# Four-stage block on one core: row scalings of the first stage on ScalarE, and new order tables for the state loops

## The reference

```python
x = x + layernorm(L0_attn(layernorm(x)))     # state-space layer
x = x + layernorm(L0_ffn(layernorm(x)))      # 8 experts, top 2, and a shared one
x = x + layernorm(L1_attn(layernorm(x)))     # differential attention
x = x + layernorm(L1_ffn(layernorm(x)))      # attention and experts with mixed weights

def layernorm(x): return (x - mean(x)) / sqrt(var(x) + 1e-5)   # over the 128 values of a row

# L0_attn, 256 channels d, 16 states n
u, z = split(x @ W_in.T)
uc = silu(conv1d(u, 3 taps) + conv_b)
B, C, dt = split(uc @ W_xproj.T);  delta = softplus(dt @ W_dt.T + b_dt)
h[n, t] = exp(delta * A[n]) * h[n, t-1] + delta * uc * B[n];  y = sum_n h[n] * C[n] + uc * D
out = (y * silu(z)) @ W_out.T

# L0_ffn, hidden size 512
combine = top-2 of softmax(x @ gate_w.T), normalized
out = sum_e combine[e] * (gelu(x @ W1[e] + b1[e]) @ W2[e] + b2[e]) + shared expert
```

## Time and profile before

| what | value |
|---|---|
| median of three runs | 2823.01 us |
| the profiled execution | 2826.37 us, of which the span is 2824.6 |
| mean granted TensorE clock | 0.876 of full speed |
| PE busy | 2196.3 us (78%), 15570 instructions |
| PEld busy | 1492.3 us (53%) |
| DVE busy | 2127.1 us (75%), 3677 instructions |
| ACT busy | 1699.0 us (60%), 2627 instructions |
| POOL busy | 1528.9 us (54%), 1343 instructions |
| L1300, VectorE's reduction of 128x1024 in the attention, x512 | mean 1215 ns |
| L791, TensorE's first up product of 128x512, x288 | mean 419 ns |
| ACT_TABLE_LOAD, x108 in the program | 1283 ns each |

### The profile page before, as it was taken

How to read it: one execution, slowest core, us unless ns; L and a number is a source line. 1 busy time by engine, 2 the same in 40 slices (tenths; PEclk the granted TensorE clock), 3 DMA queues, 4 the chain that set the end, 5 groups by cost and what they waited for, 6 DMA issues and landing times.

```text
span 2824.6 us, 42372 instructions
## 1 busy us (share of the span) xinstructions
PE 2196.3 (78%) x15570; PEld 1492.3 (53%) x15570; DVE 2127.1 (75%) x3677; ACT 1699.0 (60%) x2627; POOL 1528.9 (54%) x1343
## 2 busy tenths in 40 slices
PE   2433788588589697989889888989896799739877
PEld 1101456255356475656556566656664568536665
DVE  4999978978978514999999999999998431572344
ACT  5353666477457344989888888888894134212422
POOL 0435323523433202878987887788788524553146
PEclk7555889698689898999999999999997899869988
DMA  3000000000000000110000000011010000000000
GB/s 108 0 0 0 1 0 1 1 1 1 19 1 1 18 6 12 34 25 23 24 24 24 24 24 23 24 30 28 24 35 23 1 1 1 1 15 1 1 1 16
DMA packets 32032, 42.06 MB, mean 15 GB/s; under 512 B 8897, under 2 KB 18130, under 8 KB 31442
## 3 DMA queue, kind: packets, MB, share of 16 engines
q1 hardware_dynamic: 31826, 39.34, 5.2%
HBM read 12.05 MB, written 2.10 MB: 5 GB/s over the span
## 4 chain that ended last, share of the span: by engine, by line
PE 37%; DVE 35%; ACT 12%; issue 8%; POOL 7%; SPq 0%; DMA 0%; POOLq 0%; ACTq 0%; DVEq 0%
DVE MA L1300 11%; PE ps L862 7%; DVE WB L1309 5%; PE ps L791 3%; ACT HR L763 3%; PE ps L793 2%; PE ps L792 2%; PE ps L1161 2%; PE ps L1132 2%; PE ps L1985 2%; DVE lnb L317 2%; DVE BIG L336 2%; ACT BIG L448 2%; DVE BIG L342 2%; PE ps L1144 2%
## 5 line engine op out<-in xcount | busy, mean ns | idle before, releaser
L1300 DVE TENSOR_REDUCE MA<-ps 128x1 f32<-128x1024 f32 x512 | 606.3, 1215 | 42.6 <-PE ps L1132 38.5
L420 POOL TENSOR_TENSOR MA<-MA,BIG 128x1024 f32<-128x1024 f32 x128 | 299.0, 2357 | 544.1 <-DVE BIG L342 544.1
L1228 ACT ACTIVATE WB<-ps,MA 128x1024 f32<-128x1024 f32 x461 | 513.4, 1117 | 114.9 <-DVE MA L1300 102.6
L1132 PE MATMUL ps<-BIG 96*128 96x512 f16 x1024 | 316.1, 391 | 95.3 <-ACT WB L1228 84.3
L1380 POOL TENSOR_SCALAR WB<-WB,MA 128x384 f32<-128x384 f32 x256 | 371.1, 1450 | 8.5
L862 PEld LDWEIGHTS ps<-WB,HR 128*128 128x128 f32 x2304 | 291.6, 202 | 33.8 <-issue 16.7
L862 PE MATMUL ps<-WB,HR 128*128 128x128 f32 x2304 | 300.4, 288 | 8.7 <-DVE acc L707 8.5
L763 ACT ACTIVATE HR<-ps,b 128x512 f32<-128x512 f32 x288 | 190.2, 686 | 148.9 <-PE ps L793 148.0
L1732 POOL TENSOR_TENSOR BIG<-MA,BIG 128x512 f32<-128x512 f32 x128 | 132.9, 1048 | 229.6 <-PE ps L1971 76.1
L1144 PE MATMUL ps<-ident,WB 128*128 128x128 f32 x1640 | 226.2, 282 | 9.8 <-DVE WB L1309 5.7
L1383 POOL TENSOR_TENSOR WB<-WB 128x384 f32<-128x384 f32 x205 | 209.3, 1021 | 17.1
(11 more groups left out here) (294 smaller groups left out, 4962.3 us busy)
## 6 DMA issues: line engine op xcount, KB each, us to landing
BIG<-BIG SPq DMA_DIRECT2D x192, 64.0 KB, 2.0
BIG<-MA SPq DMA_DIRECT2D x192, 64.0 KB, 2.0
WB<-w_dram SPq DMA_DIRECT2D x1, 2304.0 KB, 14.9
X<-x_dram SPq DMA_DIRECT2D x4, 512.0 KB, 12.6
HR<-w_dram SPq DMA_DIRECT2D x1, 2048.0 KB, 9.5
out_dram<-X SPq DMA_DIRECT2D x4, 512.0 KB, 3.2
BIG<-wqkv_dram SPq DMA_DIRECT2D x1, 1536.0 KB, 6.2
WB<-w_dram SPq DMA_DIRECT2D x2, 512.0 KB, 5.1
```

What stands on the lines that cost most here:

```text
L420: e.tensor_tensor(yy[:, c, :], yy[:, c, :], db[n % 2][c], ALU.add).then_inc(*p_my.up(b, n, c))
L1132: x = e.matmul(ps[s][:, 512 * h:512 * h + 512], stack[q % 2][0:96, 0, 2 * pp + s, 128 * i:128 * i + 128], stack[q % 2][0:96, 1, 2 * pp + s ...
L1228: e.activation(P_of(n, s), ps[s][:, :], ACT.Exp, bias=L[:, 2 * s + pp:2 * s + pp + 1], scale=1.0, accum_out=L[:, 4 + 2 * s + pp:5 + 2 * s ...
L1300: e.tensor_reduce(L_of(n)[:, c:c + 1], ps[s][:, :], AX, ALU.max, negate=True).then_inc(*v_amx.up(n, s))
```

## The change

The sixteen groups of eight L317 in the first stage go from VectorE to ScalarE. ScalarE computes factor * x + shift in one activation (Identity with per-row scale and bias), for which GpSimd makes the shift, -mean * factor, with two more operations on 128x8 values after the 1/sqrt. The semaphores of the norms change their owner (`v_mln` becomes `a_mln`, `v_fln` becomes `a_fln`), and a few waits are added that guard the small tiles. All tables of planned times are new, so pieces move on every engine. The attention and the last block keep their L317 on VectorE; they gain only guards at their first use. A part of the diff (of the tables, two of thirteen):

```diff
-IN_AT = {"stats": 59.8, "norm": 72.1, "tr": 75.4, ..., "conv1": 98.3, "silu": 101.5, "wx": 104.5, ...}
+IN_AT = {"stats": 61.3, "norm": 68.5, "tr": 75.3, ..., "conv1": 91.5, "silu": 96.7, "wx": 101.6, ...}
-LOOP_AT = {"tb": -3.75, "scan1": 2.72, "scan0": 4.94, "th": 7.2, ..., "z": 20.8, "zK": 1.47, "za": -0.43}
+LOOP_AT = {"tb": -0.76, "scan1": 2.84, "scan0": 4.1, "th": 7.79, ..., "z": 18.68, "zK": -4.54, "za": 4.8}
...
+        def scale_shift(e, s):
+            rstd(e, s).then_inc(*pool_own.up())
+            e.tensor_scalar(s[:, :, 7:8], s[:, :, 6:7], -1.0, None, ALU.mult).then_inc(*pool_own.up())
+            e.wait_ge(*pool_own.now())
+            return e.tensor_tensor(s[:, :, 8:9], s[:, :, 7:8], s[:, :, 9:10], ALU.mult)
+
+        def normalized(e, s, src, dst):
+            for j in range(8):
+                i = e.activation(dst[:, j, :], src[j], ACT.Identity, bias=s[:, j, 8:9], scale=s[:, j, 9:10])
+            return i
...
         def front_dve(e, b):
             yield in_at(b, "stats")
+            last = m_order.index((b, "in")) - 1
+            if last >= 0:
+                e.wait_ge(*p_mrs.at(*m_order[last]))
             stats(e, st["m"], ...).then_inc(*v_mst.up(b, "in"))
-            yield in_at(b, "norm")
-            e.wait_ge(*p_mrs.at(b, "in"))
-            if b >= 2:
-                e.wait_ge(*p_mx.at(b - 2))
-            norms(e, st["m"], [tile_of(b, j) for j in range(8)], lnb[0]).then_inc(*v_mln.up(b, "in"))
...
         def front_pool(e, b):
             e.wait_ge(*v_mst.at(b, "in"))
-            rstd(e, st["m"]).then_inc(*p_mrs.up(b, "in"))
+            last = m_order.index((b, "in")) - 1
+            if last >= 0:
+                e.wait_ge(*a_mln.at(*m_order[last]))
+            scale_shift(e, st["m"]).then_inc(*p_mrs.up(b, "in"))
...
         def front_act(e, b):
+            yield in_at(b, "norm")
+            e.wait_ge(*p_mrs.at(b, "in"))
+            if b >= 2:
+                e.wait_ge(*p_mx.at(b - 2))
+            normalized(e, st["m"], [tile_of(b, j) for j in range(8)], lnb[0]).then_inc(*a_mln.up(b, "in"))
...
         def back_act(e, b):
+            yield out_at(b, "norm")
+            e.wait_ge(*p_mrs.at(b, "out"))
+            normalized(e, st["m"], [lnb[0][:, j, :] for j in range(8)], lnb[0]).then_inc(*a_mln.up(b, "out"))
...
         def moe_act(e, b):
+            yield f_at(b, "norm")
+            e.wait_ge(*p_frs.at(b, "in"))
+            if b:
+                e.wait_ge(*p_fx.at(b - 1))
+            normalized(e, st["f"], [tile_of(b, j) for j in range(8)], lnb[1]).then_inc(*a_fln.up(b, "in"))
             yield f_at(b, "tr", 1.2)
...
+            yield f_at(b, "rnorm")
+            e.wait_ge(*p_frs.at(b, "out"))
+            normalized(e, st["f"], [acc[:, j, :] for j in range(8)], lnb[1]).then_inc(*a_fln.up(b, "out"))
```

More of the change, by code:

```diff
@@ L96 @@
[L96 to L103, removed]
@@ L104 @@
-F_AT3 = {"stats": 0.08, "norm": 4.85, "tr": 8.6, "flo": 10.35, "gate": 11, "top": 12.79, "e": 15.58, "wts": 19.21,
-         "cT": 19.28, "k": 16.29, "K": 6.29, "up": 0.56, "dn": 6.03, "dnj": 0.78, "ge": 0.82, "done": 8.09,
-         "add": 1.73, "end": 132.4, "rnorm": 139, "x": 148.2}
+IN_AT0 = {"stats": -0.58, "norm": 1.89, "tr": 7.85, "u": 12.93, "tap0": 16.6, "tap1": 15.13, "conv0": 14.42,
+          "conv1": 22.1, "silu": 21.6, "wx": 23.8, "bc1": 26.4, "bc2": 27.8, "wdt0": 29.5, "wdt1": 35, "exp": 36.6,
+          "sp0": 40.2, "ln0": 39, "dl0": 42.9, "sp1": 40.1, "ln1": 49.1, "dl1": 51.2, "du": 52.2}
@@ new lines @@
+F_AT0 = {"stats": 2.45, "norm": 5.53, "tr": 7.35, "flo": 9.3, "gate": 8.76, "top": 17.44, "e": 20.7, "wts": 19.24,
+         "cT": 25.9, "k": 17.92, "K": 8.73, "up": 0.9, "dn": 3.84, "dnj": 1.42, "ge": 1.13, "done": 10.47,
+         "add": 11.98, "end": 186.4, "rnorm": 193.8, "x": 189.7}
+F_AT2 = {"stats": -1.4, "norm": 7.56, "tr": 12.5, "flo": 13.31, "gate": 17.42, "top": 22.6, "e": 24.1, "wts": 26.6,
+         "cT": 26.4, "k": 17.68, "K": 8.28, "up": 0.65, "dn": 6.1, "dnj": 0.26, "ge": 0.92, "done": 11.51,
+         "add": 7.2, "end": 172.8, "rnorm": 173.7, "x": 177.8}
@@ L107 @@
+F_AT3 = {"stats": -0.54, "norm": 3.84, "tr": 1.58, "flo": 14.87, "gate": 11.29, "top": 11.76, "e": 15.6, "wts": 9.85,
+         "cT": 19.46, "k": 13.36, "K": 6.65, "up": 1.05, "dn": 12.94, "dnj": 0.67, "ge": 0.43, "done": -0.33,
+         "add": 7.21, "end": 136.6, "rnorm": 137.1, "x": 135.5}
 F_AT = [F_AT0, F_AT0, F_AT2, F_AT3]
-LOOP_AT = {"tb": -3.75, "scan1": 2.72, "scan0": 4.94, "th": 7.2, "add": 9.43, "da": 0.34, "rows0": 4.86,
-           "rows1": 12.09, "z": 20.8, "zK": 1.47, "za": -0.43}
@@ L429, in back_pool @@
             e.wait_ge(*v_mst.at(b, "out"))
-            rstd(e, st["m"]).then_inc(*p_mrs.up(b, "out"))
+            last = m_order.index((b, "out")) - 1
+            if last >= 0:
+                e.wait_ge(*a_mln.at(*m_order[last]))
+            scale_shift(e, st["m"]).then_inc(*p_mrs.up(b, "out"))
             yield out_at(b, "x")
-            e.wait_ge(*v_mln.at(b, "out"))
+            e.wait_ge(*a_mln.at(b, "out"))
             xb = X[:, 8 * b:8 * b + 8, :]
@@ L657, in moe_dve @@
             yield f_at(b, "stats")
+            if b:
+                e.wait_ge(*p_frs.at(b - 1, "out"))
             stats(e, st["f"], [tile_of(b, j) for j in range(8)], {0: p_mx.at(b)}).then_inc(*v_fst.up(b, "in"))
-            yield f_at(b, "norm")
-            e.wait_ge(*p_frs.at(b, "in"))
-            if b:
-                e.wait_ge(*p_fx.at(b - 1))
-            norms(e, st["f"], [tile_of(b, j) for j in range(8)], lnb[1]).then_inc(*v_fln.up(b, "in"))
             yield f_at(b, "flo")
@@ L1272, in attend_dve @@
                     if b == 0:
[L1273 removed]
+                        e.wait_ge(*p_mrs.at(NB - 1, "out"))
                     for j in range(8):
@@ L1365, in attend_pool @@
                 e.wait_ge(*v_ast[0].at(b))
+                if b == 0:
+                    e.wait_ge(*a_mln.at(NB - 1, "out"))
                 rstd(e, st["m"]).then_inc(*p_ars[0].up(b))
```

53 lines of the change are left out of this document (29 added, 24 removed).

## The result

The changed kernel takes 2796.94 us (median of 9 runs, 2792.45 to 2802.04) against 2820.41 (median of 9, 2808.29 to 2827.39) for the kernel before. The ratio is 0.9922, with a 95% interval of 0.9905 to 0.9938: 22 us faster by the ratio, 23 by the medians. The prediction had 2826 as its likeliest time, a range of 2802 to 2845, and a chance of 0.51 for no difference.

A forecast was written before the change was run, and what follows sets the result against it. VectorE's freed time was held worthless in expert stretches; in handovers only the serial chain to L802 counts. Terms +1.7 - 1.3 - 0.8 + 7 - 10 + 0.5 + 4 + 1.8 = +2.9 on median 2823.0 gave 2826 us; range 2802 to 2845.

The forecast's parts named there:

- The group on ScalarE: Eight scalings on ScalarE, forecast at 3.2 us, bounds 2.2 and 3.8; 1.1 us longer than VectorE's group.
- The pair where GpSimd is free: GpSimd's added negation and product per group: 0.6 us where VectorE is idle, 1.0 where it is busy.
- The opening: First group, at 24.01 us, is on the chain: 0.6 + 1.1 = +1.7 us.
- The input group beside the second expert: Next batch's input group between third and fourth Gelu of the second expert, beside the shared expert's down products: costs nothing.
- rival B: Input group not covered: fourth Gelu late, TensorE waits and falls to lower level; 8 us a batch, 2842 us; chance 0.18.
- The tail: Serial chain before the last batch's experts: their start comes 4 us later, bounds +1 and +7.
- The handovers: Handovers 1 and 2: Silu load and L514s behind ScalarE's group delay the output scaling, +3.5 us each, +7 together.
- the expert stretches: Batches 0 and 1: moving the Silu pair removes TensorE's wait, -5 us each, -10 together; bounds 0 and -8 each.
- "+0.5" for batch 2: Expert stretch of batch 2: top-2 behind both scans and products, combining weights later by under 1 us: +0.5.
- A: Rival: VectorE is the bound wherever the chain names L317, nine groups from 126 to 766 us; -22, 2801 us; chance 0.27.
- C: Rival: the Silu is moved but TensorE's wait stays; 2836 us; chance 0.10.
- 12.9 without the Silu: The forecast's sum of +2.9 us with the Silu's -10 in the expert stretches left out.

The follow-up runs named there:

- experiment 7: 18 extra TensorE products fill a wait for a Gelu in the experts of batches 0 and 1, in the kernel before: 2813.18 us, ratio 0.9982.
- experiment 2: Changed kernel with the old tables of planned times, so scaling on ScalarE alone: 2834.76 us, ratio 1.0062 to the kernel before.
- experiment 1: Kernel before with the changed kernel's tables of planned times, scaling still on VectorE: 2790.38 us, ratio 0.9906.
- experiment 10: New tables with scaling on VectorE, and the experts' output scaling planned earlier ("rnorm" 193.8 to 190.2): 2778.10 us, ratio 0.9855 to the kernel before.

## Why the prediction was wrong, step by step

**Right.** The group on ScalarE (3.18 us; 3.2). The pair where GpSimd is free (0.26 + 0.21 and two gaps; 0.6). The opening: the first L568 moved from 26.30 to 27.73, +1.4 (+1.7). The input group beside the second expert costs nothing: the group at 310.83 lies where ScalarE has time, and rival B's stall does not show. The mechanism of the handovers, that the output scaling stands behind z's Silu, and that VectorE's freed time becomes waiting. The tail, +3.6 (+4). TensorE's wait of 4.49 us ahead of 354.65 is gone.

**Mis-sized.** The handovers: +6.2 and +6.3 instead of +4.6 each by these marks. The rest is GpSimd's small operation that lasts 1.9 us longer behind a scan. In the kernel before no such operation or product meets an SBUF scan in a handover: the earlier trace rows show the mean of L300 at 250 ns.

**The step that failed** is the expert stretches: "I take -5 each (4.5, and 0.5 of the slow products)", and "+0.5" for batch 2. They gave -15.6, -15.6 and -11.9. I priced the wait of 4.5 us that the moved Silu removes, and 0.5 of slow products right behind it, read from the row at 354.65. The wait was about right. The 0.5 is the term that failed: by the estimate above the time at the lower level gave 12, 10 and 7 us in the three stretches. I did not ask which other parts of the stretch ran at the lower level. The rows had it: I used the very pair 411.76 and 311.99 to price rival B's *new* gap, and did not turn it round to see that 411.76 is a slow part already there, that begins at a wait that the new order could remove. The granted clock of 0.87 in the earlier trace rows says the same: with a clock halved for part of the time, 0.13 missing over 193 us are 50 us at the lower level, up to 25 us of time. For batch 2 I looked at the VectorE order of the top-2 and counted a delay, not at the products from 782 to 811 us, nearly all at the lower level. Nor did I ask how far the three executions of the kernel before differ, 2810 to 2826, and at what clock each ran; I took their median as a fixed start.

The Trainium skill, TensorE: Matmul & The Clock Gate, HAM oscillation, states that a TensorE that waits long enough between bursts is throttled and starts the next one cold. The direction agrees with experiment 7, where the wait was filled and the products behind it came at 1.16 us instead of 2.08. The traces do not agree that the length of the wait decides, nor, as the prediction had it, that any new gap costs more than its length: the wait in the changed kernel at the same place was 2.98 us and the products behind it were at the full level, while 2.30 us in the kernel before was followed by 17 us at the lower one. First the kernel before, then the changed one:

```profile
408.58 0.39 PE L791 MATMUL ps<-xT,WB 128*128 128x512 f16 x1 [2.30 <-ACT HR L763]
409.19 0.63 PE L793 MATMUL ps<-xT,WB 128*128 128x512 f16 x1
```

```profile
400.25 0.39 PE L820 MATMUL ps<-xT,WB 128*128 128x512 f16 x1 [2.98 <-ACT HR L792]
402.06 1.16 PE L891 MATMUL ps<-WB,HR 128*128 128x128 f32 x8
```

**The rivals.** A came near the time (2801) by luck and was wrong in cause: VectorE's freed 34 us bring nothing in a stretch, and the handovers became longer. B did not happen. C (the wait stays) did not either. The sum was made of a fair list of costs and of a gain far too small. Its 12.9 without the Silu is close to the 13.9 of experiment 2, which has the costs alone, but in part by luck: there the handovers cost more than forecast, and the second stretch, by chance, gave 5.7 back.

**Still open.** Why the level falls behind one wait and not behind another of the same length in the same order; the runs show only that it differs between two stretches of one execution, and their times and clocks that it differs between executions. So it is not shown either why the new order has fewer such parts, only that it does, and what they cost. And what the input group on ScalarE is worth by itself in the stretches was not tried.

## What to carry to other kernels

When an edit changes the order, read the times of one kind of product through the whole stretch before you price it: where they are doubled, the engine's clock is low, and a part like that can be worth more than every wait in the list. Look at the single executions too: where one kernel's own differ by more than the gain that is looked for, one profile of it is not the kernel. Split a change that moves work *and* changes the order into its two halves first: here the half that had the idea in it cost 14 us alone (7 on top of the new tables), and the half that looked like mere adjustment gave 30. Taking work from a busy engine pays only where that engine's end is waited for; VectorE, busy for 89% of the window from 291 to 484 us of the changed kernel, beside a TensorE that it waits for, is not the bound there.

## What the runs showed of the hardware

VectorE's scans and scalings from SBUF to SBUF and GpSimd's work on SBUF take turns. In experiment 1, GpSimd's product pair took 6.64 us instead of 4.65, and VectorE's scan and scaling beside it 4.28 and 4.10 instead of 2.27 and 2.12.

```profile
494.97 4.28 DVE L337 TENSOR_TENSOR_SCAN BIG<-BIG 128x1024 f32<-128x1024 f32 x1
499.18 4.10 DVE L318 TENSOR_SCALAR lnb<-lnb,st_m 128x128 f32<-128x128 f32 x8
494.76 6.64 POOL L421 TENSOR_TENSOR MA<-MA,BIG 128x1024 f32<-128x1024 f32 x2
```

GpSimd's first product (2.35 us) was under way when the scan was issued, and the scan ends one product and one scan later; GpSimd's second product (4.33 us from 497.06) waits for the scan and VectorE's scaling for that product. The same holds for the smallest operation: in the changed kernel a negation of 128x8 values took 2.23 us (0.26 alone), from 481.42 to 483.65, and a scan held VectorE from 481.33 to 483.60.

```profile
481.33 2.27 DVE L349 TENSOR_TENSOR_SCAN BIG<-BIG 128x1024 f32<-128x1024 f32 x1
481.42 2.23 POOL L319 TENSOR_SCALAR st_f<-st_f 128x8 f32<-128x8 f32 x1
```

The scan and the products with an operand in PSUM do not do this: L343's pair took 2.34 us from 503.19, beside GpSimd's 2.35 from 503.35. The Trainium skill, SBUF — State Buffer, Who interferes with whom, describes the pair of ports that the two engines share as held for a whole instruction; the times agree. One number that moves a scaling by 4 us ahead of its collision brought 12 us of median (experiment 10 against 1), of which the profiles show 4 in each of two handovers. The other 4 are not shown; the two series ran on two chips and at mean granted clocks whose medians are 0.893 and 0.890.

The second thing not expected is how much one program differs by the level alone: 10.9 us between two stretches of the same order in one execution, and 24 us between executions of the kernel before, whose mean granted clock goes from 0.886 in the shortest to 0.875 in the longest.
